# One fp32 product in place of three 16-bit terms for the broadcast of C's rows in a state-space stage

## What is computed

```python
xc = conv_b + sum((xp[:, k:k + L, :] * conv_w[:, k] for k in range(Dc)))
x = jax.nn.silu(xc)
delta = jax.nn.softplus(x @ wd1.T @ wd2.T + wd2_b)
Bm, Cm = x @ wB.T, x @ wC.T                  # 16 values each per token
def step(h, inp):
    xt, dt, bt, ct = inp
    h = jnp.exp(dt[:, :, None] * A) * h + (dt * xt)[:, :, None] * bt[:, None, :]
    return h, jnp.einsum('ben,bn->be', h, ct)
```

## Time and profile before

| what | value |
|---|---|
| runs of the kernel | 2693.53 us median of 3 (2690.57 to 2693.56) |
| the profiled execution | 2695.5 us, span 2693.7 us |
| `mamba`'s steps | first scan at 860.51 us, last product at 1866.96 us |
| granted clock of PE, whole span | 0.938 |
| busy share of the span | PE 80%, DVE 72%, ACT 51%, POOL 43% |

### The profile page before, as it was taken

The page is one execution under the profiler, slowest core; times in us unless marked ns, Lnnn a source line. Parts: engine busy times, 40 slices in busy tenths (PEclk is TensorE's granted clock), DMA queues, the critical chain, the costliest instruction groups (busy, mean ns, idle before and its releaser), DMA issues. The chain is left out here.

```text
span 2693.7 us, 34646 instructions
## 1 busy us (share of the span) xinstructions
PE 2148.6 (80%) x10642; PEld 1541.2 (57%) x10642; DVE 1952.0 (72%) x2745; ACT 1374.4 (51%) x2317; POOL 1155.9 (43%) x741
## 2 busy tenths in 40 slices
PE   2799999999836777887878787766799999999940
PEld 0577877777712323333323232323799999999940
DVE  6655555655421999898989898997688888888834
ACT  1332323333225766676757666632666666666620
POOL 1211222211215989989898989883000000000036
PEclk7899999999966999999999999999899999999975
DMA  6011001111011212222222222221655555655555
GB/s 245 16 40 39 12 27 39 39 39 39 27 43 54 100 59 100 80 91 76 98 76 100 82 89 84 82 96 38 264 220 209 209 214 224 226 221 210 196 164 164
DMA packets 115029, 298.50 MB, mean 111 GB/s; under 512 B 16820, under 2 KB 89540, under 8 KB 96148
## 3 DMA queue, kind: packets, MB, share of 16 engines
q1 hardware_dynamic: 108820, 280.97, 28.8%
q0 software_dynamic: 6144, 16.79, 1.9%
HBM read 247.45 MB, written 50.27 MB: 111 GB/s over the span
## 5 line engine op out<-in xcount | busy, mean ns | idle before, releaser
L1004 POOL TENSOR_TENSOR m_work<-m_ux,m_bb 128x1024 f32<-128x1024 f32 x256 | 598.5, 2355 | 22.2 <-DVE m_hh L1199 19.3
L1283 PE MATMUL m_y<-m_work,m_ident 128*128 128x512 f32 x1024 | 495.2, 606 | 1.5 <-DVE m_work L1205 1.5
L1144 ACT ACTIVATE m_da<-m_dl,m_A 128x512 f32<-128x512 f32 x512 | 348.3, 685 | 288.8 <-DVE m_hh L1199 288.0
L1768 POOL DMA_INDIRECT c_ya<-scratch_yg,c_dst x64 | 68.2, 1066 | 733.4 <-DMA c_wts<-scratch_wts 714.3
L1199 DVE TENSOR_TENSOR_SCAN m_hh<-m_da,m_work 128x512 f32<-128x512 f32 x256 | 298.4, 1207 | 107.6 <-POOL m_work L1004 107.0
L1699 PE MATMUL e_h<-e_xTh,e_w1h 128*128 128x256 f32 x1248 | 356.5, 286 | 16.8 <-DVE e_xTl L1635 16.8
L1699 PE MATMUL e_h<-e_xTh,e_w1l 128*128 128x256 f32 x1248 | 352.2, 282 | 0.0
L1699 PE MATMUL e_h<-e_xTl,e_w1h 128*128 128x256 f32 x1248 | 352.1, 282 | 0.0
L1205 DVE TENSOR_TENSOR m_work<-m_hh,m_cb 128x1024 f32<-128x1024 f32 x256 | 312.6, 1221 | 31.1 <-PE m_cb L1264 6.9
L1199 DVE TENSOR_TENSOR_SCAN m_hh<-m_da,m_carry,m_work 128x512 f32<-128x512 f32 x256 | 313.8, 1267 | 26.6 <-POOL m_work L1004 26.6
L1283 PEld LDWEIGHTS m_y<-m_work,m_ident 128*128 128x128 f32 x1024 | 198.6, 194 | 153.9 <-issue 141.7
(11 more groups left out here) (249 smaller groups left out, 4658.1 us busy)
## 6 DMA issues: line engine op xcount, KB each, us to landing
e_w<-in_w SPq DMA_DIRECT2D x39, 2048.0 KB, 7.5
m_bb<-scratch_bT SPq DMA_DIRECT2D x64, 1024.0 KB, 4.7
e_w<-in_w SPq DMA_DIRECT2D x39, 1024.0 KB, 9.5
e_xg<-scratch_xg SPq DMA_DIRECT2D x39, 256.0 KB, 9.6
scratch_yg<-e_yo SPq DMA_DIRECT2D x39, 256.0 KB, 9.7
scratch_xg<-x1p SPq DMA_DIRECT2D x19, 512.0 KB, 7.6
e_b<-in_b SPq DMA_DIRECT2D x39, 128.0 KB, 8.6
xt<-in_x SPq DMA_DIRECT2D x9, 512.0 KB, 5.6
```

The source lines that it names most:

```text
L1004: pool.tensor_tensor(bx[:, u % NB], ux[q % 2][:, cols], slot.to_broadcast([P, HALF, T]), ALU.mult).then_inc(s_bx, 1)
L1144: act.activation(da[d % NA][:], dl[q % 2][:, e], ACT.Exp, scale=A[:, at:at + 1]).then_inc(s_exp, 1)
L1283: last = mm(y[:, i], ident[:], hc[:, u % 4, i], start=False, stop=(n % NST == NST - 1))
L1768: pool.indirect_dma_start(ya[:, a, :], None, dram["yg"][:, :], bass.IndirectOffsetOnAxis(ap=dst[:, a:a + 1], axis=0)).then_inc(yj[c], 16)
```

## The change

The rows stay in fp32. `drb` becomes two buffers of 96 rows (64 low-rank rows, then 16 of B and 16 of C), one per parity of the chunk. The selector becomes fp32 and is used in its rows 64 to 95. `spread` multiplies those 32 rows of the selector by the 32 rows of B and C, in fp32. The 16-bit copy, the two rounded copies and the two subtractions are gone, with their semaphores, and so is the wait for `s_low` in `take_step`. Two constants (`EXT`, `REC`) are added that nothing in the stage uses.

```diff
-        sel = sb("sel", [3 * 2 * NST, NST], BF16)
+        sel = sb("sel", [DR + 2 * NST, NST])
...
-        bc3 = [sb(f"bc3{h}", [3 * 2 * NST, T], BF16) for h in range(2)]
-        bc2 = spare[DR:DR + 2 * NST, 1, KE - 2].bitcast(BF16)[:, 0:T]
+        drb = [sb(f"drb{h}", [DR + 2 * NST, T]) for h in range(2)]
...
-                if n == 13:
-                    pool.wait_ge(s_row, p + 1)
-                    pool.wait_ge(s_hi, p + 1)
-                    alone(q, n)
-                    pool.tensor_tensor(bcr, brow, bc3[p % 2][DR:DR + 2 * NST], ALU.subtract).then_inc(s_res, 1)
-                    pool.wait_ge(s_res, p + 1)
-                if n == 17:
-                    pool.wait_ge(s_mid, 2 * p + 2)
-                    alone(q, n)
-                    pool.tensor_tensor(bc3[p % 2][0:2 * NST], bcr, bc2, ALU.subtract).then_inc(s_low, 1)
-                    pool.wait_ge(s_low, p + 1)
...
-                if p >= 1:
-                    act.wait_ge(b_out, 16 * p)
-                    act.wait_ge(s_low, p)
                 if p >= 2:
+                    act.wait_ge(b_out, 16 * (p - 1))
                     act.wait_ge(s_cb, (p - 1) * NU)
-                act.activation(brow, rb[DR:DR + 2 * NST], ACT.Copy).then_inc(s_row, 1)
-                act.activation(bc3[p % 2][DR:DR + 2 * NST, :], rb[DR:DR + 2 * NST], ACT.Copy).then_inc(s_hi, 1)
-                act.activation(dr, rb[0:DR], ACT.Copy).then_inc(drained, 1)
+                act.activation(drb[p % 2][DR:DR + 2 * NST], rb[DR:DR + 2 * NST], ACT.Copy).then_inc(s_row, 1)
+                act.activation(drb[p % 2][0:DR], rb[0:DR], ACT.Copy).then_inc(drained, 1)
-
-            def take_rest(p):
-                act.wait_ge(s_res, p + 1)
-                act.activation(bc2, bcr, ACT.Copy).then_inc(s_mid, 1)
-                act.wait_ge(s_mid, 2 * p + 1)
-                act.activation(bc3[p % 2][2 * NST:4 * NST, :], bc2, ACT.Copy).then_inc(s_mid, 1)
...
-                if e == HALF:
-                    act.wait_ge(s_low, p + 1)
...
                 if n == 0:
-                    pe.wait_ge(s_low, q + 1)
-                    pe.wait_ge(s_hi, q + 1)
-                    pe.wait_ge(s_mid, 2 * q + 2)
+                    pe.wait_ge(s_row, q + 1)
...
-                mm(cb[:], sel[:, at:at + 1].to_broadcast([3 * 2 * NST, P]), bc3[q % 2][:], start=True, stop=True).then_inc(s_cb, 1)
+                mm(cb[:], sel[DR:DR + 2 * NST, at:at + 1].to_broadcast([2 * NST, P]), drb[q % 2][DR:DR + 2 * NST], start=True, stop=True).then_inc(s_cb, 1)
```

More of the change, by code:

```diff
@@ L63 @@
 TMAX = NTOK // S
+EXT = 4
+REC = D + EXT
 FMS = 4
@@ L803, in mamba @@
         y1 = [[spare[:, 0, 0:HALF], spare[:, 0, HALF:KE]], [sb("y1", [P, HALF, T])[:]] * 2]
-        bcr = spare[DR:DR + 2 * NST, 1, KE - 1]
         pk = spare[:, 2:4]
@@ L809, in mamba @@
         ux = [sb(f"ux{h}", [P, KE, T]) for h in range(2)]
-        drb = sb("drb", [DR + 2 * NST, T])
-        dr = drb[0:DR]
-        brow = drb[DR:DR + 2 * NST]
-        bc3 = [sb(f"bc3{h}", [3 * 2 * NST, T], BF16) for h in range(2)]
-        bc2 = spare[DR:DR + 2 * NST, 1, KE - 2].bitcast(BF16)[:, 0:T]
+        drb = [sb(f"drb{h}", [DR + 2 * NST, T]) for h in range(2)]
         diag = sb("diag", [P, KE, P])
@@ L835, in mamba @@
                                                          sem("s_hc"), sem("s_y"))
-        s_y1, s_diag, s_hi, s_res, s_mid, s_low = (sem("s_y1"), sem("s_diag"), sem("s_hi"), sem("s_res"), sem("s_mid"),
-                                                   sem("s_low"))
+        s_y1, s_diag = sem("s_y1"), sem("s_diag")
         block = ctx.enter_context(nc.Block())
@@ L883, in store_b @@
                 sp.wait_ge(s_row, p + 1)
-                sp.dma_start(bT[p], brow[0:NST]).then_inc(b_out, 16)
+                sp.dma_start(bT[p], drb[p % 2][DR:DR + NST]).then_inc(b_out, 16)
             def load_b(G):
@@ L934, in _ @@
             pool.memset(sel[:], 0.0).then_inc(s_sel, 1)
[L935 to L938, removed]
+            pool.wait_ge(s_sel, 1)
+            pool.affine_select(out=sel[:], in_=sel[:], compare_op=ALU.not_equal, fill=1.0, base=-(DR + NST),
+                               pattern=[[-1, NST]], channel_multiplier=1).then_inc(s_sel, 1)
             pool.memset(xpad[:, :, 0:PAD], 0.0).then_inc(s_pad, 1)
@@ L946, in conv @@
                 pool.tensor_tensor(cv[:, e], taps[:, 0], taps[:, 1], ALU.add).then_inc(s_cv, 1)
[L948 to L956, removed]
             def extra(q, n):
@@ L1113, in extra @@
                         take_rows(p)
-                    if n == 14:
-                        take_rest(p)
                     if n in (14, 16, 18, 20):
@@ L1218, in _ @@
             pe.wait_ge(s_id, 2)
-            pe.wait_ge(s_sel, 4)
+            pe.wait_ge(s_sel, 2)
             pe.wait_ge(s_diag, KE)
@@ L1238, in piece @@
                     wait_drained(pe, "BD", p)
-                    last = mm(rb[:], w_dt[:, e * P:(e + 1) * P], dr, start=True, stop=True)
+                    last = mm(rb[:], w_dt[:, e * P:(e + 1) * P], drb[p % 2][0:DR], start=True, stop=True)
                 else:
```

## The result

The changed kernel took 2713.26 us in the median of 4 runs (2708.86 to 2715.56), the kernel before 2692.05 in 4 runs (2688.84 to 2693.56): a ratio of 1.0078, 95% interval 1.0061 to 1.0096. The forecast was 2706.5 in a range of 2699 to 2716. Sign and range hold, and the size fell short: +13 forecast, +21 in the runs, +18.1 between the two profiled executions (2695.5 and 2713.6 us; spans 2693.7 and 2711.7).

What follows compares the result with a forecast made beforehand. DVE was taken to bound each chunk until n = 23, then POOL. Terms -1.1 + 11.0 + 1.8 + 1.0 + 1.3 = +14.0, less 1 for the clock, gave 2693.5 + 13 = 2706.5 us, range 2699 to 2716.

Steps and rivals of the forecast that it cites:

- The two halves of a chunk: DVE bounds each chunk until n = 23; then POOL, released by ACT's L1128, to about n = 11 of the next.
- O1: PE piece at n = 22: next product some 2.1 us late, absorbed by POOL waits except in the last chunk, +1.8 us.
- O0: PE piece at n = 20: makes the product of n = 22 late by 1.50 or 1.68 us in seven chunks, +11.0 us.
- Removed work: POOL's subtractions and ACT's activations cost nothing in the chunks; the chain ahead of the first scan gains 1.1 us.
- The cost of the product: fp32 broadcast on PE: 1.05 us behind an idle PE, 1.15 behind a busy one, result after 1.12.
- n = 16: DT piece delays y of n = 15, costing about 0.1 us in each of eight chunks, +1.0 us.
- The first steps: Chunk 0 at half clock: products 1.9 us late, plus 0.9 with SK pieces, half absorbed by POOL, +1.3 us.
- The clock: Four m_cb waits behind 1.2 GHz stretches may go (-3.8 us) or lengthen (+5); -1 taken by choice.
- No drain: Rival, chance 0.2: the product on PE costs only 0.86 us, total +9.4, about 2703 us.
- Not absorbed: Rival, chance 0.2 with worse clock: O1 in six chunks and IN add too, +29, 2722 us; longer half-clock waits +19.
- Faster by the removed work: Rival, chance 0.04: POOL's removed work counts and the chunk follows POOL throughout, about 2686 us.
- Nothing to measure: Rival, chance 0.09: PE hides the fp32 product; only the start and half-clock waits move, near 2693 us.

Runs made afterwards that it cites:

- e5: The change with O0 given out in two halves behind n = 20 and 21, O1 whole; stage 1022.3 us, ratio 1.0054.
- e6: The change with O1 given out in two halves behind n = 22 and 23, O0 whole; stage 1025.0 us, ratio 1.0066.
- e2: The change with the old copies and subtractions still made, into a buffer nobody reads; stage 1024.1 us, ratio 1.0057.
- e3: The kernel before without the splitting, only the first 16-bit term kept, product still over 96 rows; stage 1006.9 us, ratio 0.9996.
- e1: The change with the fp32 product over all 96 rows, selector zero in the first 64; stage 1016.4 us, ratio 1.0024.
- e4: e3 with the 16-bit product over 32 rows instead of 96; stage 1008.3 us, ratio 1.0000.
- e9: The change with O0 halved, O1 one step later and ACT's take-out L1059 moved behind L1089; stage 1019.1 us, ratio 1.0046.
- e12: The kernel before with e9's order and six unused filler products on PE ahead of the first step; stage 1006.8 us, ratio 1.0004.
- e7: The change with O0 and O1 both in halves, behind n = 20 to 23; stage 1021.4 us, ratio 1.0055.
- e10: e9's rearrangement on top of e1's fp32 product over 96 rows; stage 1007.5 us, ratio 0.9999.
- e11: e10 with eight unused filler products on PE between the first broadcast and the first step; stage 1006.9 us, ratio 1.0000.

## Why the prediction was right, and where its sizes were off

**The two halves of a chunk: right.** The POOL half is the same in all fourteen kernels, and e5 and e6 show what it means: halving O1 takes 0.5 us off the stage, all of it in the last chunk, and halving O0 shortens six releases by 3.3 us and the stage by 3.1. POOL's wait ahead of L951 rose from 6.83 to 9.19 us (forecast +4, measured +2.4). What I had too low is how much the POOL half takes in: `m_cb` waits of 61.7 us instead of about 40, and 2.6 us of waits for POOL left in chunk 4 instead of about 5. The SK pieces and n = 0, costed at nothing, make DVE wait 3.8 us in each chunk (n = 0 to 8 of chunk 4). It cost nothing there, but it used up slack.

**Removed work, costed at nothing in the chunks and -1.1 at the start: right.** The start of the kernel ahead of BD varies by some 3 us between executions, so that the 1.25 us between the two first scans (860.51 and 859.26) agree by luck. Measured from the first copy behind BD, the removed work gains 1.25 us (41.67 to 40.4), and the change 2.2, the rest by a higher clock at the second DT piece. e2 and e3 show nothing more in the chunks.

**The cost of the product, 1.05 and 1.15 us with a result after 1.12: right.** Broadcast and `y` back to back take 2.97 us: 1.05 to `y`, 1.82 for `y`, 0.10 before the next one. Before, they took 1.94, so it is 1.03 more; by the prediction's terms it was 1.05 + 1.72 + 0.1 = 2.87, which had `y` 0.10 too short. e1 and e4 show that 0.39 us of it (0.29 in 16 bit) come from the 32 rows between products of 128. The Trainium skill (TensorEngine Tiling (Array Packing), Key Properties) says that a change of tiling mode drains TensorE, and these rows agree with it.

**O0, +11.0: right, with 12.1 measured.** The product of n = 22 is late by 1.5 to 2.1 us per chunk (forecast 1.50 and 1.68). Chunks 1 to 6 lengthen the release by 6 x 1.75 = 10.5, and the last chunk adds 1.6. That the lateness is O0's is shown by e5 and e9, where the product of n = 22 is in time.

**O1, +1.8: right.** It is 2.0 late in each chunk, taken in by the POOL half in all but the last.

**n = 16, +1.0: right in sum by luck.** It is 0.5 us in chunk 0, 0.2 in chunks 2, 4 and 6 and nothing in the odd ones, 1.1 in all, where I had 0.1 in every chunk. The INs cost 0.5 and 0.3 instead of 0.35 and 0.1, and are absorbed, as forecast.

**The first steps, +1.3: this is the term that failed.** From the first scan to the product of n = 21 chunk 0 took 83.45 us before and 87.17 after, +3.7. The timeline of the changed kernel:

```profile
863.08 2.04 PE L1223 MATMUL m_cb<-m_drb,m_sel 32*128 32x512 f32 x2 [11.19 <-DVE m_work L1166]
865.05 3.78 PE L1240 MATMUL m_y<-m_xs,m_diag 128*128 128x512 f32 x4
868.62 2.39 PE L1242 MATMUL m_y<-m_work,m_ident 128*128 128x512 f32 x4
870.85 1.88 PE L1192 MATMUL m_rb<-m_xr,m_w_si 128*128 128x512 f32 x4
872.66 1.12 PE L1223 MATMUL m_cb<-m_drb,m_sel 32*128 32x512 f32 x2
...
873.82 1.22 DVE L1166 TENSOR_TENSOR m_work<-m_hh,m_cb 128x1024 f32<-128x1024 f32 x1 [5.07 <-PE m_cb L1223]
...
912.76 1.22 DVE L1166 TENSOR_TENSOR m_work<-m_hh,m_cb 128x1024 f32<-128x1024 f32 x1 [1.66 <-PE m_cb L1223]
```

The broadcast of 2.04 us at the 1.2 GHz level is as forecast. The product of n = 2 waits 5.07 instead of 2.51 us, +2.6, and the three products behind SK pieces (n = 4, 6, 8) come 0.5 later each: 4.1 us late by n = 8, where 2.8 was forecast. POOL takes 1.2 of it back, no more, because all that DVE waited for it in this chunk before was 1.11 us (at 903.32, shown under e12). "Which I let absorb half" is the first place where the term went wrong. The second is BD, which I had costed at nothing because DVE waits for POOL there. In chunk 0 that wait was now used up, the product of n = 12 waits 1.66 us (912.76), and 1.25 us more are lost (1.66 less a wait of 0.44 for ACT that is gone). n = 17 adds 0.5 (counted above as well), and the wait of 1.06 us that the kernel before has at n = 18 is gone: -1.0. Together 4.1 - 1.2 + 1.25 + 0.5 - 1.0 = 3.7.

**The clock, -1 as a choice: about level.** The three small waits at n = 18, behind 1.2 GHz stretches, are gone, and with them 0.7 us in each of chunks 3 and 5 and 1.0 in chunk 0; the fourth lies behind a release and counts for nothing. But a new one came in chunk 1, at its BD piece, which took 2.0 back. Stretches and rows of the changed kernel:

```profile
1024.00:1028.00 4.00, 2.39 (x7) 0.72 (x5) 3.84 (x4) 2.11 (x3) 3.81 (x4) 1.00 0.15 44
1028.00:1032.00 4.00, 4.00 (x7) 1.26 (x8) 3.43 (x3) 1.28 (x2) 3.92 (x3) 0.76 0.48 153
1032.00:1036.00 4.00, 4.00 (x5) 1.38 (x5) 2.42 (x2) 3.98 (x3) 4.00 (x3) 0.50 0.38 113
```

```profile
1033.71 3.55 PE L1242 MATMUL m_y<-m_work,m_ident 128*128 128x512 f32 x4
...
1037.10 3.60 PE L1196 MATMUL m_rb<-m_xs,m_w_x 128*96 128x512 f32 x8
...
1041.78 1.22 DVE L1166 TENSOR_TENSOR m_work<-m_hh,m_cb 128x1024 f32<-128x1024 f32 x1 [2.06 <-PE m_cb L1223]
```

Ahead of it, from 1024 to 1028, PE was busy for 2.39 of 4 us at full clock. In both stretches behind that it is busy throughout, and the granted clock is 0.76 and 0.50, the 1.2 GHz level, and the product behind BD waits 2.06 us: n = 11 to 21 takes 39.93 us instead of 37.92, +2.0. The wait is there in four other kernels with 32 fp32 rows (e5, e6, e7, e9), and absent in all with 96 rows and also in e2, which has 32; so 2.0 of the +19.0 may be an event of the profiled execution and not of the change itself. What makes the clock fall there was not isolated.

The sum as measured is 10.5 (release) + 3.6 (O0 and O1 in the last chunk) + 3.7 (chunk 0) + 2.0 (BD in chunk 1) less some 0.9 for the rest (the waits at n = 18 and 16 in chunks 2 to 6) = 18.9, against 19.0 from the two traces. The two profiled executions differ by 5 us more than the +13: 3.3 of it is BD in chunks 0 and 1, which had no term, 1.6 the products of n = 2 to 8 in chunk 0, 1.1 O0, and the small waits that are gone take 1.4 off.

**The rivals.** *No drain*: falls, by the 1.05 us and by e1, which is its kernel in effect. As a forecast of e1 it was good: its stage is +10.0, with 1.25 us off at the start, near the +9.4 that I gave it, and the runs say +6.5. *Not absorbed*: falls, by e6; but e9, with 1.1 us of slack left in chunk 4, shows that the reserve was nearly spent. *Faster by the removed work*: falls, by e2 and e3. *Nothing to measure*: falls for the change, and e10 shows what it would have needed.

## What to carry to other kernels

Before making an operation longer on an engine that is not the bound, look for the places where it stands behind a long piece: there its length and the piece's add, and here two thirds of the loss came from one such place in each chunk. Count the delays that are taken in as well, against the waits that take them in: here 8.6 us a chunk shrank to 2.6, and in chunk 0, where there was 1.1, they came through. A product with fewer rows was 0.39 us dearer among products of 128; pad it with zero rows to the shape of its neighbours (ratio 1.0024 instead of 1.0078 here). And when a wait is taken from one engine, look at what the piece's other reader is queued ahead of: e5 only handed the wait from DVE to ACT, and it took a change of ACT's order (e9) to gain it.

## What the runs showed of the hardware that I had not expected

- The 32-row product costs its follower too: `y` behind it lasts 1.98 us instead of 1.88, in fp32 (1468.19) and in 16 bit (1.99 in e4), and one shape among another costs 0.39 and 0.29 us for the pair.
- The granted clock fell to 0.50 in a stretch in which the profile has PE busy for 4.00 of 4.00 us (chunk 1, 1032 to 1036), so the busy share of a row does not say which level a stretch is at. The records are longer there: 3.55 us for `y` at 1033.71, 1.98 at full clock.
- The clock that the filler products of e11 had held (1.00 from 850 to 854) was lost over an idle time of 4.93 us (0.53 from 858 to 862).
